# A layer of gated linear attention and a rank-64 mixture of experts: ScalarE rounds half of a normalized row

## The reference, cut to what matters

```python
xn = _layernorm(x)                                   # per token, over the 512 features
s  = attention_layer(xn, ...)                        # gated linear attention, then an MLP
# the mixture of experts, 8 experts of rank 64:
h     = relu(einsum('bsd,de->bse', xn, W1) + b1)
alpha = softmax(einsum('bse,ek->bsk', h, W2) + b2)
vx    = einsum('krd,bsd->bskr', V, xn)
uvx   = einsum('kdr,bskr->bskd', U, vx)
g     = silu(einsum('bsk,bskd->bsd', alpha, uvx))
out   = x + s * g
```

## Time and profile before

| | us |
|---|---|
| time, median of 3 runs | 1687.07 |
| lowest and highest of the 3 | 1685.18, 1690.03 |
| the profiled execution's own time | 1681.19 |
| its span in the trace | 1679.5 |
| busy: PE, PEld | 1617.3 (96%), 1281.6 (76%) |
| busy: DVE, ACT, POOL | 859.0, 555.6, 163.9 |

### The profile page before, as it was taken

How to read it: one execution, slowest core, us unless ns; L and a number is a source line. 1 busy time by engine, 2 the same in 40 slices (tenths; PEclk the granted TensorE clock), 3 DMA queues, 4 the chain that set the end, 5 groups by cost and what they waited for, 6 DMA issues and landing times.

```text
span 1679.5 us, 30626 instructions
## 1 busy us (share of the span) xinstructions
PE 1617.3 (96%) x12274; PEld 1281.6 (76%) x12274; DVE 859.0 (51%) x1327; ACT 555.6 (33%) x963; POOL 163.9 (10%) x190
## 2 busy tenths in 40 slices
PE   6999999859999999999999899999999999999998
PEld 5777777647777777777777688888888888888886
DVE  5565455326877778788787344141414224141413
ACT  4333333216546456356474331111111111111111
POOL 4650000020201021011110000000000000000000
PEclk9999999979999999999999999999999999999998
DMA  8434333010102102022022443020030303030100
GB/s 164 117 122 86 75 95 85 34 63 2 58 0 81 56 25 81 0 81 81 0 101 71 132 155 146 1 96 35 20 111 0 131 0 131 0 131 0 69 32 26
DMA packets 50699, 113.16 MB, mean 67 GB/s; under 512 B 13321, under 2 KB 24665, under 8 KB 42466
## 3 DMA queue, kind: packets, MB, share of 16 engines
q1 hardware_dynamic: 47906, 99.95, 18.5%
q0 software_dynamic: 1600, 4.25, 1.4%
q10 hardware_dynamic: 1152, 8.39, 1.2%
HBM read 78.98 MB, written 33.59 MB: 67 GB/s over the span
## 4 chain that ended last, share of the span: by engine, by line
PE 75%; issue 2%; DVE 1%; ACT 1%; PEld 0%; PEldq 0%; POOL 0%; DVEq 0%; ACTq 0%; POOLq 0%
PE m_ps L1361 9%; PE m_ps L1359 9%; PE m_ps L1360 9%; PE a_ps L122 7%; PE a_ps L124 7%; PE a_ps L123 7%; PE m_ps L1373 5%; PE m_ps L1375 5%; PE m_ps L1374 5%; PE a_att L1134 3%; PE a_ps L1246 2%; PE a_ps L1155 2%; PE a_ps L1241 1%; PE m_ps L1716 1%; PE a_ps L1204 1%
## 5 line engine op out<-in xcount | busy, mean ns | idle before, releaser
L1359 PE MATMUL m_ps<-m_xshi,m_w 128*128 128x512 f32 x680 | 267.9, 394 | 0.0
L1361 PE MATMUL m_ps<-m_xshi,m_w 128*128 128x512 f32 x680 | 266.3, 392 | 0.0
L1360 PE MATMUL m_ps<-m_xslo,m_w 128*128 128x512 f32 x680 | 266.2, 392 | 0.0
L1591 DVE TENSOR_TENSOR m_h<-m_ps,m_silu 128x512 f32<-128x512 f32 x85 | 58.7, 691 | 403.7 <-PE m_ps L1361 403.7
L1655 ACT ACTIVATE m_silu<-m_ps 128x512 f32<-128x512 f32 x85 | 50.8, 598 | 334.1 <-PE m_ps L1361 334.1
L1361 PEld LDWEIGHTS m_ps<-m_xshi,m_w 128*128 128x128 f32 x680 | 127.5, 188 | 28.7
L1360 PEld LDWEIGHTS m_ps<-m_xslo,m_w 128*128 128x128 f32 x680 | 127.6, 188 | 28.4 <-issue 0.2
L1359 PEld LDWEIGHTS m_ps<-m_xshi,m_w 128*128 128x128 f32 x680 | 127.6, 188 | 28.2 <-issue 0.2
L970 POOL TENSOR_TENSOR row<-row,a_r 128x512 f32<-128x512 f32 x36 | 56.6, 1602 | 399.2 <-DMA a_r<-scratch_r 399.2
L910 DVE TENSOR_TENSOR a_a<-a_att,causal 128x1024 f32<-128x1024 f32 x64 | 75.2, 1217 | 11.9 <-PE a_att L1134 11.8
L1373 PE MATMUL m_ps<-m_h0hi,m_w 128*128 128x512 f32 x192 | 75.3, 392 | 0.0
(11 more groups left out here) (276 smaller groups left out, 3499.2 us busy)
## 6 DMA issues: line engine op xcount, KB each, us to landing
row<-scratch_xn SPq DMA_DIRECT2D x16, 1024.0 KB, 4.9
row<-scratch_xmid SPq DMA_DIRECT2D x16, 1024.0 KB, 7.3
m_xt<-in_L_attn_W SPq DMA_DIRECT2D x33, 256.0 KB, 3.0
f_xt<-in_L_attn_x SPq DMA_DIRECT2D x32, 256.0 KB, 8.0
scratch_xn<-row SPq DMA_DIRECT2D x8, 1024.0 KB, 9.2
scratch_gate<-row ACTq DMA_DIRECT2D x8, 1024.0 KB, 3.9
scratch_xmid<-row SPq DMA_DIRECT2D x8, 1024.0 KB, 3.9
row<-scratch_gate SPq DMA_DIRECT2D x8, 1024.0 KB, 10.5
```

The costliest lines, as they stand in the source:

```text
L1359: pe.matmul(ps, wh, xh, start=k == 0, stop=False)
L1360: pe.matmul(ps, wh, xl, start=False, stop=False)
L1361: ins = pe.matmul(ps, wl, xh, start=False, stop=k == LAST)
L1591: dve.tensor_tensor(h[n], dense.region(f"b{j}"), silu[n], ALU.mult).then_inc(dense.taken_sem(f"b{j}"), 1)
```

## The change

The high parts of slices 2 and 3 are written by ScalarE and no longer by VectorE. ScalarE does it as an activation (Copy) from the same tile into the same tile, after the evictions of alpha0 and of alpha1 respectively; for row 0 it does both right after its evictions of the normalized row. VectorE still rounds slices 0 and 1, and before it subtracts in slices 2 and 3 it waits for ScalarE's semaphore `xnhi_act`. ScalarE's part waits, as VectorE's did, until the matmuls of v3 have read the old high parts. TensorE's program is unchanged.

```diff
-                          ("xnhi", KT), ("xnlo", KT), ("softmax", 5), ...
+                          ("xnhi", HALF), ("xnhi_act", KT - HALF), ("xnlo", KT), ("softmax", 5), ...
@@ VectorE
                 for m in range(KT):
-                    dve.wait_ge(*turn.taken(f"xn{m}", i))
-                    dve.tensor_copy(xn_hl[0][:, m, :], xn[:, m, :]).then_inc(count.sem("xnhi"), 1)
-                    dve.wait_ge(*count.at("xnhi", i, m + 1))
+                    if m < HALF:
+                        dve.wait_ge(*turn.taken(f"xn{m}", i))
+                        dve.tensor_copy(xn_hl[0][:, m, :], xn[:, m, :]).then_inc(count.sem("xnhi"), 1)
+                        dve.wait_ge(*count.at("xnhi", i, m + 1))
+                    else:
+                        dve.wait_ge(*count.at("xnhi_act", i, m - HALF + 1))
                     dve.tensor_tensor(xn_hl[1][:, m, :], xn[:, m, :],
                                                     xn_hl[0][:, m, :].bitcast(F32), ALU.subtract).then_inc(count.sem("xnlo"), 1)
@@ ScalarE
+            def split(i, m):
+                act.wait_ge(*dense.ready_before(f"v{LAST}", i))
+                act.wait_ge(*turn.taken(f"xn{m}", i))
+                act.activation(xn_hl[0][:, m, :], xn[:, m, :], ACT.Copy).then_inc(count.sem("xnhi_act"), 1)
...
                 for m in range(KT):
+                    if 0 < m <= KT - HALF:
+                        ahead(f"split{HALF + m - 1}")
                     act.wait_ge(*turn.ready(f"alpha{m}", i))
                     act.activation(alpha_b[:, m, :], turn.region(f"alpha{m}"), ACT.Copy).then_inc(turn.taken_sem(f"alpha{m}"), 1)
...
-            loop_parts(act, NB, {"norm": norm, "xn": fill_xn, "b1": first_bias, "h": hidden}, body)
+            loop_parts(act, NB, {"norm": norm, "xn": fill_xn, **{f"split{m}": lambda i, m=m: split(i, m) for m in range(HALF, KT)},
+                                 "b1": first_bias, "h": hidden}, body)
```

More of the change, by code:

```diff
@@ L317, in phase_f @@
         for name, per in (("stats", TT), ("mv", TT), ("rstd", 2), ("m2", 2), ("r1", 2), ("norm", TT),
-                          ("xnhi", KT), ("xnlo", KT), ("softmax", 5), ("exp", 1), ("partial", 1), ("alpha", 1), ("vxhi", KT),
+                          ("xnhi", HALF), ("xnhi_act", KT - HALF), ("xnlo", KT), ("softmax", 5), ("exp", 1), ("partial", 1), ("alpha", 1), ("vxhi", KT),
                           ("vxlo", KT), ("xn_out", 16), ("r1_out", 16),
```

## The result

| | us |
|---|---|
| before, median of 7 runs (lowest, highest) | 1686.84 (1681.65, 1690.03) |
| changed, median of 7 runs (lowest, highest) | 1676.47 (1674.47, 1681.03) |
| ratio of the two, with its 95% interval | 0.9946 [0.9929, 0.9963] |
| the profiled execution's own time, before and changed | 1681.19 and 1676.47 |
| its span, before and changed | 1679.5 and 1674.7 |

By the ratio the change is faster by 0.54%, some 9 us (the two medians lie 10.4 us apart); 0.38% was forecast, inside the interval, just at its lower edge of 0.37%. The two profiled executions are only 4.8 us apart. Both facts need explaining.

What follows compares the result with a forecast made beforehand. TensorE was held by VectorE's rounding and subtraction in each row's first output of `hidden`. Gains of 4.5 + 1.5 + 0.4 = 6.4 us from 1687.07 gave 1680.7 us, range 1677.0 to 1686.0.

Steps and rivals of the forecast that it cites:

- The chain: VectorE's rounding copies and subtractions, for which TensorE waits in h0; two copies fewer end slice 3's subtraction 0.91 us earlier.
- its price and its cover: Two ScalarE copies per row, 0.63 us each, priced at nothing; narrowest margin 0.2 us, plus 0.3 us of TensorE's slack.
- three terms of the sum: Rows 1 and 3 to 7 at 0.75 us each, 4.5 us; row 2, 1.5 us; row 0, 0.4 us.
- The bound: In h0, VectorE's rounding plus subtraction sets the pace of k1 to k3, 1.06 to 1.07 us apart instead of 0.69.
- What TensorE makes of it: In h0, k2 and k3 follow k1 without a stop, so h1 starts 0.75 us earlier, not 0.91.
- the rest becomes slack: What remains of the 0.91 us beyond 0.75 is no gain, as TensorE is the bound again before h1.
- What hides the additions: ScalarE's two copies fit among the four evictions of the turned alpha, ready 0.68 and 0.2 us before VectorE wants them.
- Row 0: First row, TensorE at 0.43 us a matmul: gain taken as 0.4 us, bounds 0.15 and 0.75.
- Row 2: Row where GpSimd held VectorE's copy of slice 2: gain taken as 1.5 us, bounds 0.75 and 1.88.
- The 2 us allowed for the clock: Allowance of 2 us either way on the total, for shifting stretches where TensorE runs at 0.50 of its clock.
- the rival that part is given back: ScalarE is late or row 2 stays held: gain only 3.2 us, so 1683.9 us; chance 0.16.
- 2.2 us from k1 to h1: Sign: from h0's second step of three matmuls (k1) to the next output (h1), 2.2 us instead of 2.94.

Runs made afterwards that it cites:

- quiet_after: The changed kernel, but SyncE issues no first-stage load before GpSimd has prepared the attention weights: 1752.42 us, against 1757.93 for the kernel before with the same wait.
- late: The changed kernel with ScalarE rounding slices 2 and 3 after all four evictions of alpha instead of between them: 1680.49 us, ratio 0.9962 to the kernel before.
- again: The changed kernel, unaltered, timed once more: 1677.53 us, ratio 0.9952 to the kernel before.
- three: The changed kernel with slice 1 also rounded by ScalarE, ahead of alpha0's eviction: 1675.35 us, ratio 0.9938 to the kernel before.
- before_third: The kernel before, unaltered, run for a third profile: 1688.05 us, ratio 1.0008 to the earlier runs of the kernel before.
- one_slice: The changed kernel with slice 2 left to VectorE, so ScalarE rounds only slice 3: 1682.20 us, ratio 0.9974 to the kernel before.
- three_vx: three, plus ScalarE writing the high parts of vx and VectorE forming slice m+1 of vx before subtracting in slice m: 1677.40 us, ratio 0.9942 to the kernel before.
- late_again: The kernel late, repeated unaltered: 1678.61 us, ratio 0.9955 to the kernel before.
- before_again: The kernel before, unaltered, run for a second profile: 1684.86 us, ratio 0.9995 to the earlier runs of the kernel before.
- quiet_late: The kernel late, but SyncE issues no first-stage load before GpSimd has prepared the attention weights: 1758.21 us, against 1757.93 for the kernel before with that wait.

## Why the prediction was right

The chain, its price and its cover were right. The number was right partly by luck: of the three terms of the sum, row 2's failed in the profile shown and row 0's is not told from chance.

*The bound.* TensorE waited for VectorE's rounding and subtraction. Shown: with one copy fewer h1 came 0.37 to 0.38 us sooner, with two 0.75.

*What TensorE makes of it.* The 0.75 us of the 0.91 was met in each of rows 3 to 5 (0.75, 0.74, 0.76), in row 7 (0.77) and in quiet_after. It was not in row 1, which the prediction had put with them: 0.19 there from k1 to h1. The step that said the rest becomes slack held too: VectorE's next read of PSUM came 132.81 to 133.49, and h1 followed k3 at 0.69.

*What hides the additions.* The copies came 0.49 and 1.49 us after alpha0's eviction began, as laid out (0.49 and 1.54), ended at 130.92 and 131.93, and cost nothing. A choice of the faster engine would have given the sign wrongly here, as the chain is on VectorE and the room on ScalarE; late shows that room at the wrong moment is none.

*Row 0.* 0.4 forecast, 0.70 measured up to row 1 in this pair. It is not told from chance: in the profiles beside GpSimd h0 of row 0 starts anywhere from 14.96 to 16.68 us, and of this pair only before ran its first matmuls 0.43 us apart.

*Row 2.* 1.5 forecast, 1.60 us lost in the profile shown: the step that failed in this execution. It supposed that, coming 1.2 us earlier, the row would in part miss GpSimd; it came 2.96 us earlier and met other pieces instead, from slice 1 on, and the clock fell after the stops. Its lower bound, 0.75, allowed for no loss. In again the same row took 38.80. Over the profiles rows 1 and 2 took 82.9 us on average before and 80.7 after, 2.1 us less; 2.25 had been counted (0.75 and 1.5). With a spread of 3.1 us among the three profiles of before and 2.2 among the two of the changed kernel, that agreement is luck as much as reckoning. What GpSimd costs in one row depends on how the two fall together, and the prediction had no term for the place where it cost most in row 1, TensorE's wait for the normalized row (1.25 us, then 0.20).

*The sum and the clock.* 6.4 us forecast with bounds 5.4 and 7.1; 5.5 us without GpSimd (6.4 by the ratios), 8.4 over the profiles with the clock's cost removed, 9.1 and 8.1 by the two ratios, whose intervals reach down to 6.2 and 5.4. So the sum is more likely too small than too large, by about 2 us, and what it lacks is not placed. The first pair of profiles showed 4.8 us because the changed one happened to pay 14.7 us for the half clock and the one before 12.6: 6.9 without it. The 2 us allowed for the clock were too few, it moved single executions by up to 4.8 (11.9 to 16.7 for the same kernel).

*What the signs said.* 2.2 us from k1 to h1: seen. Subtractions 0.61 apart, no wait for ScalarE: seen in the undisturbed rows. Evictions and copies in 3.2 us: 3.10. The wait for low parts falling to 4 us: 6.2, because of row 2 (3.3 in again). The first stage 6 us shorter: 4.4, for the same reason. No table load came, and h1 followed the earlier subtraction. Of the rival that part is given back, one condition appeared in this execution, a row 2 that stays held; the other, ScalarE late, did not.

*Open.* Late gained 5.6 and 7.0 us by the medians, 3.4 by its two profiles without the clock's part, and nothing without GpSimd. VectorE having fewer operations beside GpSimd in rows 0 to 2 may be some of that (rows 1 and 2: 82.9 to 81.2 us, less than the spread of before), and fewer clock drops there could be the rest; one profile per set of runs can't settle it. The same part may be in the changed kernel's 8 to 9 us; that isn't shown.

**The best version.** three has the lowest medians, 1675.35 and 1675.78 us, but its ratios are 0.9938 [0.9924, 0.9953] and 0.9935 [0.9921, 0.9948], and the changed kernel's intervals, [0.9929, 0.9963] and [0.9937, 0.9968], overlap both. Its undisturbed rows are 0.08 us shorter, worth 0.6 us in all. It isn't shown to be better.

## What to carry to other kernels

When a fast engine waits step by step for a two-operation chain on a slower one, hand one of the operations to an engine that is idle at that very moment, and lay out on the timeline when each result must be there; the same operations 1.0 to 1.4 us later brought nothing in the undisturbed rows. Count the gain at the waiting engine and not at the relieved one: 0.75 of 0.91 here. And before a difference of a few microseconds between two profiles is read as the change's, take the half clock's cost out of both, and look at the matmuls' pace as well as at the granted clock: where the engine started, the column showed 1.00 while they ran 0.43 us apart.

## What was not expected of the hardware

The clock can fall inside a stage and not only between two: from 89 to 92 us TensorE was busy 0.47, 0.46 and 0.50 of each microsecond, and a stretch at 1.2 GHz followed that cost 1.7 us. In five other profiles (before_third, one_slice, late, three, three_vx) one came in row 0 (at 17 to 19 us), costing 1.6 to 1.7 us, with and without the change. In three (before, again, late_again) the matmuls of row 0 began at that pace under a granted 1.00, costing 1.6 to 3.0 us. Over a whole execution beside GpSimd the half clock cost 11.9 us (before_again) to 16.7 us (before_third).

GpSimd's work beside VectorE adds to the spread: rows 1 and 2 of one and the same kernel took 81.5 to 84.6 us, and 78.6 without GpSimd. The Trainium skill ("SBUF — State Buffer", section "Who interferes with whom") has VectorE's copies in a two-port mode and its operations with two SBUF inputs contend with GpSimd, and ScalarE never wait. The traces agree for VectorE (1.28 instead of 0.42 us for the copy, 3.68 instead of 1.89 for three subtractions), and for ScalarE, whose copy at 87.96 us took 0.62 beside GpSimd's subtraction, and whose 16 copies in the changed kernel are alike with and without GpSimd beside them (shortest, median and longest ns):

```profile
L523 ACT ACTIVATE f_xnhi<-row x16: 621/622/632, 14.8 to 285.8; 128x512 fp32r<-128x512 f32 x16
```

In row 6 of the changed kernel the matmuls that followed each other directly were 0.232 us apart on average instead of 0.229, at a granted clock of 1.00, and the row took 0.37 us more. Row 4 in again, row 2 in quiet_after and row 7 in quiet_late did the same (0.232). What sets it isn't shown.
